# Attention and mixture-of-experts block on one core: first norm a sequence ahead, two head groups in one value bank

## The reference, cut to what matters

```
x = x + layernorm(attention(layernorm(x)))
x = x + layernorm(ffn(layernorm(x)))

scores = (Q K^T + Q rel_k[idx]) / sqrt(8), causal, softmax
out    = attn V + attn rel_v[idx];   out @ W_o + b_o
ffn    = silu(x sw1) * (x sw3) @ sw2  +  the best 2 of 8 experts, gelu(x ew1) ew2, weighted by gates
```

## Time and profile before

| | us |
|---|---|
| three runs | 1033.69, 1034.54, 1032.93 (median 1033.69) |
| profiled execution: its time | 1030.79 |
| profiled execution: span | 1029.1 |
| PE busy | 898.8 (87%) |
| DVE busy | 817.6 (79%) |
| POOL busy | 728.0 (71%) |
| ACT busy | 680.5 (66%) |
| mean granted clock of PE | 0.939 |

### The profile page before, as it was taken

How to read it: one execution, slowest core, us unless ns; L and a number is a source line. 1 busy time by engine, 2 the same in 40 slices (tenths; PEclk the granted TensorE clock), 3 DMA queues, 4 the chain that set the end, 5 groups by cost and what they waited for, 6 DMA issues and landing times. The chain is left out here.

```text
span 1029.1 us, 25739 instructions
## 1 busy us (share of the span) xinstructions
PE 898.8 (87%) x8935; PEld 526.4 (51%) x8935; DVE 817.6 (79%) x1948; ACT 680.5 (66%) x1315; POOL 728.0 (71%) x946
## 2 busy tenths in 40 slices
PE   2888988999899988998999898887679999999995
PEld 0443444544445444444444444433357777777773
DVE  4787888888888888887888888876667888878884
ACT  3247777767668777776777867665346767676773
POOL 5244686686776867768668777566257989898886
PEclk9999999989889999898899998987889999999998
DMA  3311111111111111111111111001425454545541
GB/s 82 137 34 26 29 43 28 35 46 27 29 27 38 43 28 33 40 27 35 28 36 46 28 31 37 25 26 43 162 62 156 150 170 153 164 150 166 163 138 31
DMA packets 58828, 70.88 MB, mean 69 GB/s; under 512 B 8944, under 2 KB 34416, under 8 KB 58720
## 3 DMA queue, kind: packets, MB, share of 16 engines
q1 hardware_dynamic: 56432, 69.04, 23.1%
q10 hardware_dynamic: 2288, 0.42, 0.2%
HBM read 43.75 MB, written 8.65 MB: 51 GB/s over the span
## 5 line engine op out<-in xcount | busy, mean ns | idle before, releaser
L1137 DVE TENSOR_REDUCE mx<-ps_s 128x1 f32<-128x512 f32 (+2 forms) x640 | 410.2, 682 | 75.2 <-PE ps_s L1549 74.2
L809 ACT ACTIVATE prob<-ps_e 128x512 f32<-128x512 f32 x640 | 352.0, 608 | 110.3 <-PE ps_e L1506 110.2
L651 POOL TENSOR_SCALAR_AFFINE_SELECT prob<-prob 128x516 f32<-128x516 f32 (+1 forms) x320 | 176.6, 576 | 150.2 <-ACT prob L809 150.1
L1530 PE MATMUL ps_s<-ks,qs 31*128 31x512 f16 (+3 forms) x1024 | 196.5, 324 | 32.2 <-DVE mx L1137 27.0
L1572 PE MATMUL ps_av<-prob,vp 128*32 128x512 f32 (+3 forms) x2048 | 202.5, 495 | 4.3 <-POOL prob L651 4.2
L731 POOL TENSOR_TENSOR hidden_low<-hidden,hidden_high 128x512 fp32r<-128x512 f32 x144 | 191.0, 1354 | 12.0 <-ACT hidden_high L998 10.7
L1506 PE MATMUL ps_e<-qs,ks 32*128 32x512 f16 (+3 forms) x1024 | 167.9, 316 | 6.2 <-ACT prob L809 2.0
L1530 PEld LDWEIGHTS ps_s<-ks,qs 31*128 31x128 f16 x1024 | 54.9, 94 | 167.6 <-issue 89.4
L1549 PE MATMUL ps_s<-masked_at,below 32*128 32x64 bf16 (+3 forms) x2560 | 135.0, 192 | 0.0
L998 ACT CAST hidden_high<-hidden 128x512 fp32r<-128x512 f32 x160 | 98.0, 613 | 30.7 <-DVE hidden L1450 27.5
L1549 PEld LDWEIGHTS ps_s<-masked_at,below 32*128 32x128 bf16 x2560 | 105.6, 98 | 20.0 <-issue 4.1
(11 more groups left out here) (173 smaller groups left out, 1664.3 us busy)
## 6 DMA issues: line engine op xcount, KB each, us to landing
gate_rows<-gates_dram SPq DMA_DIRECT2D x128, 256.0 KB, 3.7
qs<-qh SPq DMA_DIRECT2D x64, 64.0 KB, 2.1
xnT_dram<-oT SPq DMA_DIRECT2D x16, 256.0 KB, 2.0
xeT<-xnT_dram SPq DMA_DIRECT2D x16, 256.0 KB, 2.8
out<-result SPq DMA_DIRECT2D x16, 256.0 KB, 2.3
v_near<-v_back SPq DMA_DIRECT2D x16, 254.0 KB
ks<-kh SPq DMA_DIRECT2D x62, 64.0 KB, 2.1
qs<-ql SPq DMA_DIRECT2D x32, 64.0 KB, 2.1
```

The lines of the kernel that those rows point to most:

```text
L651: pool.affine_select(out=v, in_=v, compare_op=ALU.is_ge, fill=0.0, base=-2, pattern=cols, channel_multiplier=-1).then_inc(S["p_masked"], 1)
L809: act.activation(prob[g % 2][:, u, b, :], ps_e[bank][:, :], ACT.Exp, scale=SCALE).then_inc(S["e_done"], 1)
L1137: dve.tensor_reduce(out, src, AX.X, ALU.max).then_inc(s_free[bank], 1)
L1530: pe.matmul(scores[:, at:at + P * (qt + 1)], qs[par][rows, pr, P * qt:P * qt + P], ks[par][rows, pr, 0:P * (qt + 1)], start=(n == 0), stop ...
```

## The change

It does three things. The first norm of sequence t+1 is made in step t (on DVE `ln1_bn` at the step's start, on POOL behind `split`), and `xnT` has two buffers, so that the transpose stands in round 0, queries in 3 and keys in 5. The values move from round 5 to 8, the output projection from 11 to 9, `s_tok` from 7 to 10; on DVE `values_out` goes from behind 10 maxima to behind 16, `y_out` from 22 to 18, `x1_bn` from 30 to 29. On POOL the split stands behind 5 masks in place of 10, the second norm behind 10 in place of 12. Two groups of heads share the value bank: an even group uses columns 0 to 15 of the 32 in `vp`, an odd one 16 to 31, with zeros elsewhere, and the odd one adds to the same bank. So `av_out`, `av_transpose` and `av_tok_out` run twice a sequence and not four times, with `den` and `num` twice as wide; `v_out` is two copies of half the size. x of sequences 1 and 2 is loaded ahead of the rest.

```diff
-AT = {"e_sums": 1, "av2": 2, "m1": 4, "v0": 5, "av3": 6, "xT": 6, "s_tok": 7, "oT": 7, "q": 9,
-      "k": 10, "oproj": 11, "av0": 14, "m0": 15, "av1": 17, "xn2": 18, "logits": 19}
+AT = {"xT": 0, "e_sums": 1, "q": 3, "m1": 4, "k": 5, "av1": 6, "oT": 7, "v0": 8, "oproj": 9, "s_tok": 10,
+      "m0": 15, "av0": 17, "xn2": 18, "logits": 19}
...
-        vp = [sb(f"vp{i}", [P, NT, H, 32]) for i in range(2)]
+        vp = [sb(f"vp{i}", [P, NT * NGRP, 4, 2 * WIDE]) for i in range(2)]
...
 # POOL, step
-                masks(0, 3)
-                if st.F:
-                    normalise(st, st.f, xn[:, :, :], tiles(xr[:, st.seq(st.f), :]), mv1, var1, rs1,
-                              "stats1").then_inc(S["xn_ready"], 1)
-                masks(3, 10)
+                masks(0, 5)
                 if st.F:
                     split(st)
+                    if st.f + 1 < NSEQ:
+                        norm1(st.f + 1)
...
 # ACT
-                act.copy(vp[st.a % 2][:, :, :, 0:D].rearrange("p t h d -> p (t h) d"),
-                         ps_s[bank][:, :].rearrange("p (c d) -> p c d", d=D)).then_inc(S["v_ready"], 1)
+                of = ps_s[bank][:, :].rearrange("p (c j d) -> p c j d", j=4, d=D)
+                for q in range(2):
+                    last = act.copy(vp[st.a % 2][:, q::2, :, WIDE * q:WIDE * q + D], of[:, q::2])
+                last.then_inc(S["v_ready"], 1)
...
-            def av_out(st, s, g):
+            def av_out(st, s, part):
 
-                act.wait_ge(S["av_full"], st.at(NGRP * s + g + 1, NGRP))
-                act.copy(av_s[g % 2][:, :], ps_av[:, :]).then_inc(S["av_copied"], 1)
+                act.wait_ge(S["av_full"], st.at(NGRP * s + 2 * part + 2, NGRP))
+                act.copy(av_s[part][:, :], ps_av[:, :]).then_inc(S["av_copied"], 1)
...
 # PE, av_part
-                    last = pe.matmul(ps_av[32 * j:32 * j + 32, P * kt:SEQ], vp[par][:, kt, 4 * g + j, :],
+                    last = pe.matmul(ps_av[32 * j:32 * j + 32, P * kt:SEQ], vp[par][:, NGRP * kt + g, j, :],
                                      prob[g % 2][:, u, j % 2, at:at + w],
-                                     start=(kt == 0), stop=(kt == NT - 1))
+                                     start=(kt == 0 and g % 2 == 0), stop=(kt == NT - 1 and g % 2 == 1))
```

More of the change, by code:

```diff
@@ L208, in end @@
     def end(self):
-        if LOOP0 <= self.st.t0 < NSEQ and self.per_step != self.n - self.first:
+        if LOOP0 <= self.st.t0 < NSEQ - 1 and self.per_step != self.n - self.first:
             raise AssertionError((self.n - self.first, self.per_step))
@@ L293, in block_kernel @@
             xn = sb_front("xn", [P, NT, P])
-            xnT = sb_front("xnT", [P, 1 + SEQ])
+            xnT0 = sb_front("xnT0", [P, 1 + SEQ])
             qf = sb_front("qf", [P, SEQ])
@@ L322, in block_kernel @@
         av_s = [sb(f"av_s{i}", [P, SEQ]) for i in range(2)]
-        den = sb("den", [P, NT, 8])
-        rden = sb("rden", [P, NT, 8])
-        num = sb("num", [P, NT, 8, D])
+        den = sb("den", [P, 2, NT, 4])
+        rden = sb("rden", [P, 2, NT, 4])
+        num = sb("num", [P, 2, NT, 4, D])
         o_tok = sb("o_tok", [P, NT, P])
@@ L365, in block_kernel @@
             qs, ks = [qs0, qs1], [ks0, ks1]
+            xnT = [xnT0, xnT1]
         w_first = sb("w_first", [P, 12, P])
@@ L404, in block_kernel @@
         S = {n: sem(n) for n in names}
-        x_loaded = [S["x_loaded0"], S["x_loaded1"], S["x_loaded2"]]
+        x_loaded = [S[f"x_loaded{i}"] for i in range(4)]
         stacks = [[S[f"stacks{par}{half}"] for half in range(2)] for par in range(2)]
@@ L714, in step @@
                     selectors()
-                masks(12, 15)
+                masks(10, 15)
                 if st.t0 == NSEQ + 2:
@@ L816, in xT_out @@
                 act.wait_ge(S["e_full"], n + 1)
-                act.copy(xnT[:, 1:1 + SEQ], ps_e[bank][:, :]).then_inc(S["e_done"], 1)
+                act.copy(xnT[st.f % 2][:, 1:1 + SEQ], ps_e[bank][:, :]).then_inc(S["e_done"], 1)
             def q_out(st):
@@ L1047, in value_buffers @@
                 dve.memset(vp[i][:, :, :, :], 0.0).then_inc(S["v_rows"], 1)
-                dve.wait_ge(S["v_rows"], 2 * i + 1)
-                dve.memset(vp[i][:, :, :, D:D + 1], 1.0).then_inc(S["v_rows"], 1)
+                dve.wait_ge(S["v_rows"], 3 * i + 1)
+                for q in range(2):
+                    at = WIDE * q + D
+                    dve.memset(vp[i][:, q::2, :, at:at + 1], 1.0).then_inc(S["v_rows"], 1)
             def qk_constants():
@@ L1191, in av_tok_out @@
                 own.settle()
-                own.mark(dve.reciprocal(rden[:, :, :], den[:, :, :]))
+                own.mark(dve.reciprocal(rden[:, :, :, :], den[:, :, :, :]))
                 own.settle()
-                dve.wait_ge(S["misc_free"], st.misc(f"av{g}") + 1)
-                both = slice(4 * (g - 1) * D, 4 * (g + 1) * D)
-                dve.tensor_tensor(o_tok[:, :, both].rearrange("p t (j d) -> p t j d", d=D), num[:, :, :, :],
-                                  rden[:, :, :].unsqueeze(3).to_broadcast([P, NT, 8, D]),
+                dve.wait_ge(S["misc_free"], st.misc(f"av{part}") + 1)
@@ L1297, in maxima @@
                             s_max(st, i)
-                if st.F:
-                    ln1_bn(st)
+                after = st.t0 + 1 if 0 < st.t0 < NSEQ - 1 else None
+                if st.t0 == 0:
+                    ln1_bn(0)
+                    aggregate(st1, mv1, "stats1")
+                if after:
+                    ln1_bn(after)
                 maxima(0, 2)
@@ L1311, in step @@
                 maxima(3, 7)
-                if st.F:
+                if after:
                     aggregate(st1, mv1, "stats1")
-                maxima(7, 9)
-                maxima(9, 10)
-                if st.A:
-                    values_out(st)
-                maxima(10, 11)
+                maxima(7, 11)
                 if st.t0 == NSEQ + 2:
@@ L1330, in step @@
                     gates_second(0, EARLY)
-                maxima(13, 18)
+                maxima(13, 16)
                 if st.A:
-                    s_tok_out(st)
-                maxima(18, 22)
+                    values_out(st)
+                maxima(16, 18)
                 if st.C:
@@ L1604, in values @@
                 for i in range(NT):
-                    last = pe.matmul(u[:, i * P:i * P + P], xnT[:, 1 + i * P:1 + i * P + P], wv[:, :],
+                    last = pe.matmul(u[:, i * P:i * P + P], xnT[st.a % 2][:, 1 + i * P:1 + i * P + P], wv[:, :],
                                      start=True, stop=True)
```

176 lines of the change are left out of this document (88 added, 88 removed).

## The result

The changed kernel takes 1065.8 us (median of 4 runs, 1063.7 to 1072.9) against 1033.6 us for the kernel before: a ratio of 1.0323, 95% interval 1.0272 to 1.0374. It is 3.2% slower; 994.5 was forecast. The profiled execution took 1063.7 us, with a span of 1061.6.

A forecast was written before the change was run, and what follows sets the result against it. No engine is full; PE and DVE, handing work through three score banks, bound the step. Gains of 2.6 us over 13 full steps (34) plus 5 elsewhere made 39 us, giving a forecast median of 994.5 us, range 984 to 1006.

The forecast's parts named there:

- the cost of the new order, -0.5 - 0.2 a step: Losses per full step: 0.5 us for `values_out` in DVE's half, 0.2 us for the second group's values being late.
- rival 3: ACT's `q_out` in round 3 waits for DMAs of the previous sequence's stacks; slower, 1050 us; chance 0.06.
- The wait for `xn`, 1.3 us a step: PE's wait for POOL's first norm before the `xn` transposes, expected to go and be gained whole: 1.3 us a step.
- Transposes and pairs, 1.0 us a step: Shared bank: 0.7 us from a set of transposes PE loses, 0.3 us from wider `den` and `num` pairs on DVE.
- The wait for `xr`, 0.6: DVE's wait for POOL's `xr` before x1's statistics, expected to go with the earlier second norm: 0.6 us a step.
- PE's busy time was to fall: Expected in the new profile: PE's busy time down about 1.5 us a step, DVE's down 0.6.
- The clock, +0.4: With fewer stops PE may be granted 2.4 GHz longer: between 0 and 0.9 us a step, taken 0.4.
- rivals 1 and 3: Rival 1: holes close, but POOL is 1.5 us late at round 11, clock gives nothing; 1017 us, chance 0.18. Also rival 3.
- a sign of being wrong: The prediction called itself wrong if ACT waits before `qh` for a DMA.
- DVE's waits for scores stay at 54 us: Sign of being wrong: if DVE's summed waits for PE's scores stay at 54 us, the banks set the pace.
- 1.3 + 0.3: Gain in step 2, which has no third stage: put at 1.5 us.
- 0.7 + 0.3 + 0.6: Gain in step 16, which has no first norm: put at 1.5 us.

The follow-up runs named there:

- the layout with the transpose first: Changed kernel with queries and keys back in rounds 9 and 10, only the input transpose left in round 0: 1021.4 us, ratio 0.9894.
- the bank alone: Kernel before with only the shared value bank; norm, queries, keys, values and projection where they were: 1029.9 us, ratio 0.9970.
- the queries alone in round 3: Kernel with the input transpose in round 0 and keys in round 10, with the queries moved from round 9 to 3: 1071.6 us, ratio 1.0363.
- the run with the keys in the hole: Kernel with transpose in round 0 and queries in 3, with the keys moved from round 10 to 9, ahead of the projection: 1062.3 us, ratio 1.0265.
- The fastest kernel: Changed kernel with the transpose in round 0, queries and keys both in round 9 ahead of the projection: 1018.7 us, ratio 0.9848.

## Why the prediction was wrong

- **The step that failed: the cost of the new order, -0.5 - 0.2 a step in the sum.** It priced the moved queries only as a possible wait of ACT for DMAs (rival 3) and the moved values as 0.5 us on DVE. Two things were left out. The queries' product, 1.1 us on PE, moved to round 3, where no wait was found that it could fill. And the values, moved to round 8, made a chain of PE, ACT, DVE and PE again with 1.7 us of hole ahead of the projection in round 9. The second is cheap by itself: the values and projection in their new rounds cost 4 us while the queries, late, stand in that hole. The text said "what is late next" for the norm, and never asked it for the bank of the values. In the layout with the transpose first, the place of the queries is 50 us, from 1021.4 to 1071.6; the keys' move from 10 to 5, with split and norm on POOL, then gives back 6, down to the changed kernel's 1065.8. How much of the 50 is the hole is shown only in part: 12.6 of the 40.1 us by which the twelve steps grew are PE's wait for `v_near`, 18.2 are PE's busy time.
- **The wait for `xn`, 1.3 us a step, counted whole.** It is gone, and worth nothing: with the bank alone PE waits 13.4 us for an exponential at the same place, and with both waits gone the step is 0.16 us shorter in the profiles and the median time 6 us longer.
- **Transposes and pairs, 1.0 us a step.** The counts came out (128 transposes of `av_s`, 32 pairs), and so did the price of a pair (0.18 and 0.41 us against 0.60), but the bank alone is worth 3 us in all.
- **The wait for `xr`, 0.6.** Gone, as forecast, and covered by the larger losses.
- **PE's busy time was to fall by about 1.5 us a step and DVE's by 0.6.** Both rose, PE's from 37.3 to 38.6 and DVE's from 35.0 to 36.4; DVE's has the stretched `d` of the last section in it.
- **The clock, +0.4.** The other way: the changed kernel's full steps have 0.81 to 0.96, three of them at 0.81 or 0.85, where the twelve of before have 0.89 to 0.98. The Trainium skill, TensorE: Matmul & The Clock Gate, section What's actually happening, has the clock fall after idleness. The traces do not bear that out step by step: the same empty hole is followed by a projection of 1.97 us with the queries alone in round 3 and by one of 1.16 us in the changed kernel, and the run with the keys in the hole has less idleness before the projection and a lower clock, 0.85 against 0.88. The measurement decides; what sets the clock from step to step stays open.
- **POOL late at round 11, and the stacks' DMAs (rivals 1 and 3).** Neither happened in the full steps: PE waits for no mask, and ACT's wait before `qh` is for PE, 1.73 us. Ahead of them, within the first 144 us, ACT did wait once before `qh` for a stack's DMA, 5.7 us; the text had that as a sign of being wrong, but the full steps begin at 145.6 us against 145.3 before, so it is no part of the loss.
- The text named as a refutation that DVE's waits for scores stay at 54 us, "then the banks, and not the holes, set the pace". They rose to 68.9, so the sign did come, but no rival with a chance stood behind it. In the transpose-first run, with the same values and projection, they are 38.5. Only rival 3 ended slower, and by another mechanism.

- **Two sums are off by 0.1**: 1.3 + 0.3 and 0.7 + 0.3 + 0.6 are 1.6, not 1.5. It changes nothing.

What stays open: why the early transpose gives 18 us in the new layout; how the 27 us divide between the hole, ACT's wait and the clock, beyond the 12.6 us of the wait itself; why the steps keep one length whether the hole is filled or not; and what the values and the projection in their old rounds would give beside early queries if ACT copied the values ahead of k, which was not tried with the shared bank.

## What to carry to other kernels

An instruction that stands in another's wait is free only there. Before moving one, look at what stood behind it in its own queue, what that was waiting for, and whether anything fills the hole afterwards: here the order of two products inside one round was worth 27 us. The fastest kernel, 1.5% below the kernel before, has that order, but the step that brought it below was the transpose's move to round 0, 18 us, which is not explained. Check what filling a hole gives, too: here it gave 9 us in one run and 3 in another, because PE was busy for longer with the same instructions. And a wait that is to be removed has a next lock behind it: find its release time before counting the whole wait.

## What the hardware showed

VectorE's small `d` (128x32) took 0.19 us at the median before and 0.65 in the changed kernel, with a pair of 1.76 us at 394.17. Source view of before:

```profile
L1166 DVE SCALAR_TENSOR_TENSOR d<-m,s_tok x64: 177/191/916, 50.7 to 682.6; 128x32 f32<-128x32 f16 x64
```

Timeline of GpSimd at that time:

```profile
394.02 1.27 POOL L720 TENSOR_TENSOR xr<-xr,y 128x512 f32<-128x512 f32 x1
```

Moved away from it, the median is 0.19 again. The maxima, which read a PSUM bank, kept their length beside the same kind of work: the longest of all 640 took 0.70 us, the median 0.68. The Trainium skill, Trainium Architecture — The Big Picture, section What this means for kernel authors, speaks of a port pair that VectorE and GpSimd share under an exclusive lock; the stretch agrees with it. Curing it gained nothing here, which only the run that did so could tell.
